# Re-ordering the streams and fronts of two state-space layers, a cell layer that normalises three batches itself, and earlier norm steps in two ternary layers

## The reference, cut to what matters

```
x = x + layer_i(layernorm(x))        # i = 0 .. 15
layernorm(x) = (x - mean(x)) / sqrt(var(x) + 1e-5)     # over the 128 features of a token
```

```
xi, z = split(x @ w_in)                       # 256 channels each
u     = silu(causal_conv4(xi) + conv_b)
dt, B, C = split(u @ w_x)                     # 64, 16, 16 columns
delta = softplus(dt @ w_dt + dt_b)
for t in tokens:  h = exp(delta_t * A) * h + (delta_t * u_t) * B_t ;  y_t = sum_n h[:, n] * C_t[n]
out   = ((y + u * D) * silu(z)) @ w_out
```

## Time and profile before

| | us |
|---|---|
| median of 3 runs | 2786.97 (2784.44 to 2788.79) |
| the profiled execution | 2771.81 |
| its span | 2769.6 |
| busy PE / DVE / ACT / POOL | 2313.0 / 1745.0 / 1191.3 / 616.0 |
| mean granted clock of PE | 0.909 of full speed |
| stream of layer 10, first scan to last | 1758 to 2053 |
| stream of layer 14 | 2428 to 2722 |

### The profile page before, as it was taken

How to read it: one execution, slowest core, us unless ns; L and a number is a source line. 1 busy time by engine, 2 the same in 40 slices (tenths; PEclk the granted TensorE clock), 3 DMA queues, 4 the chain that set the end, 5 groups by cost and what they waited for, 6 DMA issues and landing times. The chain is left out here.

```text
span 2769.6 us, 29539 instructions
## 1 busy us (share of the span) xinstructions
PE 2313.0 (84%) x9664; PEld 1001.0 (36%) x9664; DVE 1745.0 (63%) x2473; ACT 1191.3 (43%) x2367; POOL 616.0 (22%) x610
## 2 busy tenths in 40 slices
PE   8999999677399989779987799677779978867777
PEld 3333334322122244454553344232234456322233
DVE  5666665578877545543645645688864556488885
ACT  3555653178277721313422343444425422344442
POOL 1111120323111100211010100455530031165551
PEclk9999999889699989988679899888799999988889
DMA  3000000122000020000000000211100000011110
GB/s 149 1 1 1 1 1 1 22 41 31 1 1 1 1 92 0 1 1 1 1 1 0 0 0 0 69 54 61 54 8 1 1 1 2 24 61 60 55 46 15
DMA packets 18822, 59.67 MB, mean 22 GB/s; under 512 B 2224, under 2 KB 8432, under 8 KB 17648
## 3 DMA queue, kind: packets, MB, share of 16 engines
q1 hardware_dynamic: 17808, 57.01, 6.6%
q10 hardware_dynamic: 864, 0.79, 0.2%
HBM read 50.12 MB, written 1.31 MB: 19 GB/s over the span
## 5 line engine op out<-in xcount | busy, mean ns | idle before, releaser
L3659 POOL TENSOR_TENSOR l_drive<-l_du,l_bsb 128x1024 f32<-128x1024 f32 x128 | 302.4, 2371 | 195.6 <-DVE l_state L3440 193.6
L3440 DVE TENSOR_TENSOR_SCAN l_state<-l_decay,l_drive 128x1024 f32<-128x1024 f32 x128 | 292.8, 2288 | 68.9 <-ACT l_decay L3406 55.6
L3282 PE MATMUL l_py<-l_read,w_const 128*128 128x512 f32 x512 | 290.9, 698 | 0.0
L402 ACT ACTIVATE l_probs<-l_psp,l_stats 128x512 f32<-128x512 f32 x256 | 173.1, 683 | 150.4 <-DVE l_stats L412 150.4
L263 POOL TENSOR_TENSOR l_nx_small<-l_nx_small,w_const 128x4 f32<-128x4 f32 x44 | 46.5, 1056 | 820.2 <-DVE l_nx_small L257 820.2
L3268 PE MATMUL l_pc<-l_parts,l_spread 96*128 96x512 bf16 x128 | 55.7, 435 | 173.8 <-DVE l_read L3450 172.1
L3406 ACT ACTIVATE l_decay<-l_delta,l_a 128x511 f32<-128x511 f32 x256 | 164.0, 680 | 81.6 <-DVE l_state L3440 81.4
L1278 DVE TENSOR_REDUCE l_tops<-l_ring 128x2 f32<-128x1024 f32 x128 | 151.5, 1221 | 45.6 <-PE l_ring L1269 45.2
L410 DVE TENSOR_REDUCE l_stats<-l_psp 128x2 f32<-128x1024 f32 x128 | 156.2, 1221 | 35.6 <-PE l_psp L364 35.1
L718 DVE SCALAR_TENSOR_TENSOR l_product<-l_psu,w_gated,l_first 128x512 f32<-128x512 f32 x104 | 78.1, 751 | 133.8 <-ACT l_first L692 133.5
L1350 ACT ACTIVATE l_shared<-l_ring 128x512 f32<-128x512 f32 x256 | 138.9, 598 | 49.4 <-PE l_ring L1340 49.2
(11 more groups left out here) (576 smaller groups left out, 4424.8 us busy)
## 6 DMA issues: line engine op xcount, KB each, us to landing
l_bsb<-l_rows SPq DMA_DIRECT2D x64, 512.0 KB, 3.5
l_stack<-l_parts SPq DMA_DIRECT2D x84, 64.0 KB
w_gated<-in_gated SPq DMA_DIRECT2D x1, 3297.5 KB, 12.3
w_mha<-in_mha SPq DMA_DIRECT2D x1, 2568.5 KB, 13.4
w_ssm<-in_ssm SPq DMA_DIRECT2D x2, 1171.0 KB, 16.3
w_moe<-in_moe SPq DMA_DIRECT2D x1, 2248.0 KB, 18.4
w_const<-in_const SPq DMA_DIRECT2D x1, 1325.0 KB, 7.7
x<-x_in SPq DMA_DIRECT2D x1, 1024.0 KB, 5.0
```

The lines of the kernel that those rows point to most:

```text
L402: act.activation(probs[:, s % 4, i, :], psp[:, s % 2, i, :], ACT.Exp, bias=stats[:, s % 4, 1, i:i + 1], scale=scale, accum_out=stats[:, s ...
L3282: mm = pe.matmul(py[:, t, :], eye, read[:, k % 2, t, :], start=False, stop=k % NS == NS - 1, skip_group_check=True)
L3440: dve.tensor_tensor_scan(state[:, k % 2, :, :].rearrange("p t s -> p (t s)"), decay[:, k % 2, :, :].rearrange("p t s -> p (t s)"), drive[: ...
L3659: pool.tensor_tensor(drive[:, k % RING, :, :], du[:, :, :], bsb[:, k // 2 % RING, k % 2, :].unsqueeze(1).to_broadcast([P, CT, S]), ALU.mult)\
```

## The change

- **State-space, PE.** `between(b, n)` is issued before `spread_c(k+1)` and `add_up(k)` instead of behind them. The delta products move from n = 7, 9 to 7, 8.
- **State-space, ACT.** `raw_x` moves from n = 3 to 4, `copy_low` from 8 to 9, magnitude and positive part from 9, 11 to 10, 11, exponential from 11 to 12, logarithm from 12 to 13. Batch 0's silu of z moves from the front to n = 6; the exponential of A moves ahead of the magnitudes.
- **State-space, DVE.** `split_parts` moves from n = 8 to 9, both `add_positive` to 13, `finish` from 13 to 14. In the front DVE copies z of batch 0 out of PSUM, makes both halves of `du` and the drive of step 0 (`drive_first`).
- **State-space, PE front.** `project_low` goes ahead of z. The norm of the previous layer's batch 3 (`late`) moves from n = 10 to 15 of batch 0 to the front, with the bank `py` in place of `front`.
- **Cell.** With `inner` > 0 it runs the norm chain for its batches 0 to 2 behind the answers; layer 13 joins `NORMALISES_NEXT` and layer 14 `NORMALISES_LAST`, so the block of its own between them goes.
- **Ternary layers.** centre from 3 to 2 products behind the batch, square and keep from 4 to 2, var from 5 to 3, eps and diag from 6 to 3, spread from 7 to 5, scale from 8 to 5.

```diff
 # state_space, stream of TensorE
                 for k in range(PAIRS):
                     b, n = divmod(k, NS)
+                    between(pe, b, n)
                     if k + 1 < PAIRS:
                         spread_c(pe, k + 1)
                     if b and n == 0:
                         for t in range(CT):
                             add_skip(pe, b, t)
                     add_up(pe, k)
-                    between(pe, b, n)
 # between
-                if n in (7, 9):
-                    project_delta(pe, b + 1, (n - 7) // 2)
+                if n in (7, 8):
+                    project_delta(pe, b + 1, n - 7)
 # state_space, front of TensorE
+                if last_in:
+                    late.centre(pe, B - 1)
                 for t in range(CT):
                     pe.wait_ge(L["taps"].sem, L["taps"].at(0, t + 1))
                     project_x(pe, 0, t, (0, 1, 2, 3))
+                    if last_in and t == 0:
+                        late.var(pe, B - 1)
+                project_low(pe, 0)
                 for t in range(CT):
                     project_z(pe, 0, t)
-                project_low(pe, 0)
+                if last_in:
+                    late.spread(pe, B - 1)
 # state_space, ScalarE
-                        if n == 3:
+                        if n == 4:
                             raw_x(act, b + 1)
...
-                        if n == 8:
+                        if n == 9:
                             copy_low(act, b + 1)
-                        if n in (9, 11):
-                            magnitude(act, b + 1, (n - 9) // 2)
-                            positive_part(act, b + 1, (n - 9) // 2)
-                        if n == 11:
+                        if n in (10, 11):
+                            magnitude(act, b + 1, n - 10)
+                            positive_part(act, b + 1, n - 10)
+                        if n == 12:
                             for t in range(CT):
                                 soft_exp(act, b + 1, t)
-                        if n == 12:
+                        if n == 13:
                             for t in range(CT):
                                 soft_log(act, b + 1, t)
 # state_space, front of VectorE
-                dve.tensor_tensor(du[:, 1, :], delta[:, 0, 1, :], u[:, 1, :], ALU.mult).then_inc(L["du"].sem, 1)
+                for t in range(CT):
+                    dve.tensor_tensor(du[:, t, :], delta[:, 0, t, :], u[:, t, :], ALU.mult).then_inc(L["du"].sem, 1)
+                dve.wait_ge(L["du"].sem, L["du"].at(0, CT))
+                dve.wait_ge(L["bsb0"].sem, L["bsb0"].at(0, 16))
+                dve.tensor_tensor(drive[:, 0, :, :], du[:, :, :], bsb[:, 0, 0, :].unsqueeze(1).to_broadcast([P, CT, S]),
+                                  ALU.mult).then_inc(L["drive_first"].sem, 1)
 # state_space, stream of VectorE
-                        if n == 8:
+                        if n == 9:
                             split_parts(dve, b + 1)
-                        if n in (12, 13):
-                            add_positive(dve, b + 1, n - 12)
-                        if b and n == 13:
+                        if n == 13:
+                            for t in range(CT):
+                                add_positive(dve, b + 1, t)
+                        if b and n == 14:
                             finish(dve, b - 1)
 # state_space, GpSimd
+                    if k == 0:
+                        pool.wait_ge(L["du"].sem, L["du"].at(0, CT))
+                        continue
 # cell, TensorE
-                for b in range(2, B):
-                    answer_input(pe, b)
-                    answer_state(pe, b)
+                answer_input(pe, 2)
+                answer_state(pe, 2)
+                if inner:
+                    pe.wait_ge(L["opened"].sem, L["opened"].at(0, 3 * B))
+                    nx.centre(pe, 0)
+                answer_input(pe, 3)
+                answer_state(pe, 3)
+                if inner:
+                    nx.centre(pe, 1)
+                    nx.var(pe, 0)
+                    nx.centre(pe, 2)
+                    nx.var(pe, 1)
+                    nx.spread(pe, 0)
+                    nx.var(pe, 2)
+                    nx.spread(pe, 1)
+                    nx.spread(pe, 2)
 # bit_ffn, TensorE
-                    if normed(n, 3) is not None:
+                    if normed(n, 2) is not None:
                         if last_in:
                             pe.wait_ge(L["in_xn"].sem, L["in_xn"].at(0, 1))
-                        nx.centre(pe, normed(n, 3))
-                    if normed(n, 5) is not None:
-                        nx.var(pe, normed(n, 5))
-                    if normed(n, 7) is not None:
-                        nx.spread(pe, normed(n, 7))
+                        nx.centre(pe, normed(n, 2))
+                    if normed(n, 3) is not None:
+                        nx.var(pe, normed(n, 3))
+                    if normed(n, 5) is not None:
+                        nx.spread(pe, normed(n, 5))
```

138 lines of the change are left out of this document (78 added, 60 removed).

## The result

The changed kernel takes 2685.05 us in the median of 4 runs (2678.52 to 2686.65) against 2785.70 for the kernel before in the same set: ratio 0.9665, 95% interval 0.9631 to 0.97. The forecast was 2701 with a range of 2688 to 2738.

The account below looks back on a forecast made before the run. VectorE paces state-space layers 10 and 14 yet waits, mostly for ScalarE's decays. Savings 39.9 + 37.0 + 0.9 + 4.5 + 4.0 = 86.3 took the profiled 2771.8 to 2685.5 us; that execution lay 15 under the median, so 2701, range 2688 to 2738.

Parts of the forecast that it names:

- Streams: Layers 10 and 14, first scan to last read-out: 39.9 and 37.0 us shorter, after the price is taken off.
- decay waits: VectorE's scans waiting for ScalarE's decays in layers 10 and 14: 26.3 and 26.1 us removed.
- the softplus sum: `add_positive` in both streams, moved to step 13 clear of GpSimd's product: 4.0 us saved in each layer.
- the price: Read-outs waiting for `pc` behind the moved products: 3.0 us lost in layer 10, 5.5 in layer 14; ends 0 and 36.
- The cast: Split's first cast in the streams: waits for `low` go, about 1.0 us of each of three stays behind GpSimd's product.
- Front of layer 10: Tap weights to first scan, with VectorE making `du` and the first product: net 0.9 us shorter; ends -1.5 and 2.7.
- the rival in which GpSimd takes the port: State-space fronts: GpSimd's product starts before VectorE's first one, 2.4 us back in each layer, 2706 us; 24 in 100.
- Seam and layer 14's front: Layer 13 to 14, norm moved into the cell: 6.1 us shorter by the working, 4.5 taken; ends 0 and 8.
- Ternary layers: Ends of layers 5 and 7, norm steps earlier: 1.9 us shorter twice, 4.0 rounded; ends 1 and 5.
- Half clock in the dense steps: Streams: TensorE falls to half clock and `pc` is late, 2729 us, or 2737 with the norm entries; 15 in 100.
- ScalarE late elsewhere: Streams: ScalarE late by 2 us at two places of six batches returns 24 us, 2725 us; 7 in 100.
- products in series: Streams: `between`'s products no longer run beside scans, 102 us added against 86 saved, 2803 us; 8 in 100.

Follow-up runs that it names:

- e7: Changed kernel with VectorE's copy of batch 2 and second diagonal ahead of batch 0's scale at the cell's end: 2685.57 us, ratio 0.9689.
- e8: As e7, plus six unread 256-column products on TensorE between the cell's last variances and spreads: 2676.80 us, ratio 0.9659.
- e2: Kernel before with the state-space edits alone, cell and ternary layers as before: 2696.39 us, ratio 0.9726.

## Why the prediction was right, and where not

- **Streams.** 39.9 and 37.0 forecast, 41.4 and 41.7 measured. The large removals came as forecast: decay waits (0.5 and none left), finish (0.5 of 4.2 left), keep, the softplus sum back to 682 ns; the undone order and the order alone show the mechanism from both sides. The term that was mis-sized is the price: 3.0 and 5.5 for `pc`, where the read-outs wait 0.5 and 0.2 for it. The feared cause was there: 16 of the 128 add-ups took 2.4 to 3.6 us instead of 1.88, in every batch and not only in batch 0, where the prediction's text puts the half clock. In the kernel before it was 38 of 128, so the prediction's counter-argument, that with the long waits TensorE's idle stretches go too, was right for most of them. The slow ones cost next to nothing. By the prediction's own working `pc` is late only where a slow add-up and a long entry meet in one step, and its upper end of 36 let them meet twice in each of six batches; they hardly ever met. Behind the stream the last gate now waits 0.96 us for the sum, which comes behind the last spread, but the last scale comes earlier by more: from the last read-out to the last addition both layers take 8.12 us instead of 8.27.
- **The cast.** 1.0 of each was to stay; 1.33 did (1748 ns against 0.41 us in the front). VectorE and GpSimd of the changed kernel in order of time:

```profile
1782.56 1.75 DVE L3449 CAST l_parts<-l_low 32x512 bf16<-32x512 f32 x1
1784.34 0.68 DVE L3451 TENSOR_TENSOR l_low<-l_low,l_parts 32x512 f32<-32x512 f32 x1
...
1781.67 2.35 POOL L3708 TENSOR_TENSOR l_drive<-l_du,l_bsb 128x1024 f32<-128x1024 f32 x1 [1.17 <-DVE l_state L3473]
```

The cast ends 0.28 behind GpSimd's product, in each of the six batches; the run that moved it shows that the wait is the place's and not the cast's. No semaphore stands between the two, so the engines do not meet only at semaphores, as the first section has it. The norm's diagonal (L270) is held in the same way: the two in each stream take 2.87 and 2.57 us instead of 0.68 and end 0.55 us behind a product of GpSimd, 4.1 us a layer. That is more than the six casts cost (8.2 us in both layers against 8.0), it was there before (2.89 each), and neither the prediction nor any run went after it.

- **Front of layer 10.** 0.9 forecast, 0.79 measured. VectorE's product, which had no row, took 1.22 (1195 ns taken), and it started 0.04 to 0.05 us ahead of GpSimd's in both layers, so the rival in which GpSimd takes the port did not come. GpSimd in the front of layer 14, beside VectorE's product at 2375.47:

```profile
2375.52 12.62 POOL L3708 TENSOR_TENSOR l_drive<-l_du,l_bsb 128x1024 f32<-128x1024 f32 x5 [14.09 <-DVE l_du L3617]
```

These five products take 1.07 more than five of 2.31, while VectorE's runs at full speed.

The Trainium skill (SBUF — State Buffer, section "SBUF: two separate sides") has the loser of the shared port blocked for the winner's whole instruction. The casts, the subtraction and the diagonals that end shortly behind GpSimd's product agree; for GpSimd's five products the loss by that rule would be 1.17 (an estimate: from their start at 2375.52 to VectorE's end at 2376.69), where 1.07 was measured.

- **Seam and layer 14's front.** 4.5 forecast, 0.8 measured (77.14 to 76.34 from the cell's start to the first scan). This is the step that failed, in two terms. The chain was given 11.4 from the old end and took 14.2. Batch 2's copy stood behind batch 0's scale on VectorE, which no step of the working had (2.3 us of the cell's stretch by e7), and its last products ran at half clock (1.5 us of it by e8). The front was given 23.8 and took 26.26, and the difference is clock: 23.93 with TensorE kept busy. The text priced half clock in the front at 1.7, which is what lies between its 6.1 and its 4.5; it was 2.3, and for the chain itself, whose gaps of 1 to 2 us the text names, it priced nothing. The stand-alone normalisation that was removed had, once started, run its products with no gap over 0.17 us and at full clock (1.00 from 2387 to 2399); the new chain has one batch less and has the gaps. By e2 the new front alone gives 2.8 us here, and the cell's chain takes 2.0 of them back.
- **Ternary layers.** 4.0 forecast, 3.3 measured.
- **Sum.** The misses, +6.2 in the streams, -3.8 in seam and fronts, -0.7 in the ternary layers, and -1.3 in the ends of layers 10 and 14 with 11 and 12 (the unedited layers 11 and 12 took 1.65 more, the two ends 0.3 less), cancel to 0.3: that 86.6 stands beside 86.3 is luck. The 6.3 us of unedited layer 6 came on top, so that the profiled execution took 2678.5 where the working had 2685.5. The median lies 16 us under the forecast, and the other 9 is nearly all the step from that execution to the median: the prediction added the 15 us by which its profiled execution lay under the median, and in the changed kernel that distance is 6.5. So the measured median fell 3 us under a range that was made from the edited parts alone, while layers without an edit move by several microseconds between programs, and layer 0 by 8 between executions.
- **Rivals.** Half clock in the dense steps, ScalarE late elsewhere, and products in series would each have left 20 us or more in front of scans or read-outs. The changed kernel has 11.8 us in front of all its scans and 2.9 in front of all its read-outs.

## What to carry to other kernels

When the engine that paces a stream waits, look at what stands ahead of the late operation in each in-order queue: one call moved in front of another on TensorE gave 30 of the 41 us of layer 10's stream, and 14 to 17 us of a stream's waits could be removed a second way. Price a chain of small dependent steps with TensorE's gaps in it: at the lower clock it and the layer behind it cost 3 us more, and fillers into a free bank took that back. Judge an edit by a stretch cut at the same instructions (0.03 us here), not by the whole time, which moved by some 20 us for reasons outside the edit. And look at operations that are long without waiting: nothing in the idle column names the 8 us that the diagonals lose beside GpSimd's products.

The version with both seam edits and ScalarE's cast, 904.42 in the stretch against 914.46 for the changed kernel on the same chip, took 2681.42 us against 2688.53; its stretch is 10.0 us shorter (1.6 of it in the unedited layers 11 and 12), and the intervals of the whole times' ratios, 0.9602 to 0.9661 and 0.9641 to 0.9695, overlap.

## What the runs showed of the hardware that was not expected

- Between programs that are the same up to layer 10, layers 2 to 5 differ by up to 6.8 us (766.9 against 760.2), and within one program they repeat to 0.6 us.
- A 32x512 subtraction to f32 in SBUF waits for GpSimd's running product as the 32x512 conversion to bf16 does: 1.91 and 1.75 us instead of 0.68 and 0.41. A 128x512 product of two SBUF inputs does so too: 2.87 us instead of 0.68.
- Six filler products of 256 columns shorten a chain of 11.1 us to 9.6, though four of them stand in front of products that the chain waits for, by keeping the granted clock at 1.00. In e7, the same chain without them, the first slow spread (2.06 us, at 2353.35) comes behind gaps of TensorE of no more than 0.60 us.
